# Ternary weights on two engines: GpSimd makes the first comparison, VectorE the second

## The reference

```
x = x + 0.5 * ffn0(ln(x))      # int weights: (w - 128) * scale, silu(gate) * up, down;  hidden 704
x = x + attn0(ln(x))           # 16 heads of 16, rotary, causal
x = x + 0.5 * ffn0(ln(x))
x = x + 0.5 * ffn1(ln(x))      # ternary weights: sigmoid(x1) * x2, then w3
x = x + attn1(ln(x))           # 16 query heads on 4 key heads, ALiBi, causal
x = x + 0.5 * ffn1(ln(x))
```

```
gamma = mean(abs(w));  q = clip(round(w / (gamma + 1e-8)), -1, 1)
```

## Time and profile before

| | |
|---|---|
| median of 3 runs | 553.93 us (552.02 to 555.36) |
| the profiled execution | 552.14 us, its span 550.4 us |
| TensorE clock granted | 1.000 over the span |
| TensorE busy | 530.6 us (96%), 5060 products |
| VectorE busy | 456.1 us (83%) |
| ScalarE busy | 401.3 us (73%) |
| GpSimd busy | 340.8 us (62%) |
| share of the DMA queue q1 | 16.4% of 16 engines |

### The profile page before, as it was taken

How to read it: one execution, slowest core, us unless ns; L and a number is a source line. 1 busy time by engine, 2 the same in 40 slices (tenths; PEclk the granted TensorE clock), 3 DMA queues, 4 the chain that set the end, 5 groups by cost and what they waited for, 6 DMA issues and landing times.

```text
span 550.4 us, 12977 instructions
## 1 busy us (share of the span) xinstructions
PE 530.6 (96%) x5060; PEld 302.9 (55%) x5060; DVE 456.1 (83%) x816; ACT 401.3 (73%) x603; POOL 340.8 (62%) x427
## 2 busy tenths in 40 slices
PE   8999798999999999999899999999999999999997
PEld 6676444445554654566446564465455654654664
DVE  5999999998989797699987969879997779783363
ACT  5978594878777698775886848788769676969443
POOL 2549896975987797673664364552855626545634
PEclk9999999999999999999999999999999999999999
DMA  8900110302130100410110120010211011101211
GB/s 324 355 1 2 58 58 2 116 23 62 41 103 18 43 1 2 157 42 20 63 43 2 42 83 22 22 43 6 75 36 43 1 42 64 52 2 62 80 58 38
DMA packets 22573, 31.76 MB, mean 58 GB/s; under 512 B 9408, under 2 KB 10816, under 8 KB 22360
## 3 DMA queue, kind: packets, MB, share of 16 engines
q1 hardware_dynamic: 22512, 30.94, 16.4%
HBM read 13.75 MB, written 2.36 MB: 29 GB/s over the span
## 4 chain that ended last, share of the span: by engine, by line
PE 71%; DVE 17%; ACT 4%; issue 3%; POOL 2%; SPq 1%; DMA 0%; DVEq 0%; POOLq 0%; ACTq 0%
PE PS L597 22%; PE PS L621 12%; PE PS L708 10%; PE PS L688 5%; PE PS L673 5%; DVE MX L1064 5%; PE PS L639 4%; PE PS L723 4%; PE PS L580 3%; PE PS L544 2%; PE PS L559 2%; ACT PB L850 2%; PE PS L655 2%; DVE MX L1060 1%; DVE ST L875 1%
## 5 line engine op out<-in xcount | busy, mean ns | idle before, releaser
L850 ACT ACTIVATE PB<-PS 128x1024 f32<-128x1024 f32 x160 | 158.7, 1025 | 52.9 <-PE PS L688 48.4
L1064 DVE TENSOR_REDUCE MX<-PS 128x2 f16<-128x1024 f32 (+2 forms) x192 | 158.3, 865 | 13.8 <-PE PS L544 13.1
L597 PE MATMUL PS<-XT,WGU 128*128 128x512 f16 x660 | 156.9, 380 | 4.6 <-DVE QF L1042 3.0
L1140 POOL TENSOR_TENSOR HH<-TH,HH 128x512 f16<-128x512 f32 x71 | 82.5, 1173 | 69.0 <-ACT HH L818 69.0
L1168 POOL TENSOR_SCALAR_AFFINE_SELECT PB<-PB 128x512 f32<-128x512 f32 (+1 forms) x140 | 73.8, 552 | 48.1 <-ACT PB L850 47.9
L597 PEld LDWEIGHTS PS<-XT,WGU 128*128 128x128 f16 x660 | 59.6, 98 | 75.9 <-issue 7.8
L621 PE MATMUL PS<-WD,HH 128*128 128x256 f16 x660 | 78.2, 273 | 0.4 <-POOL HH L1140 0.2
L708 PE MATMUL PS<-PB,V 128*32 128x512 f32 (+3 forms) x1024 | 75.3, 435 | 0.8 <-ACT PB L850 0.3
L621 PEld LDWEIGHTS PS<-WD,HH 128*128 128x128 f16 x660 | 62.6, 98 | 13.3 <-issue 3.3
L818 ACT ACTIVATE HH<-TH 128x512 f16<-128x512 f32 (+1 forms) x86 | 52.9, 628 | 20.2 <-PE PS L621 6.9
L673 PE MATMUL PS<-SK,SQ 63*128 63x256 f16 (+3 forms) x512 | 59.5, 299 | 5.3 <-DVE MX L1064 2.6
(11 more groups left out here) (119 smaller groups left out, 777.7 us busy)
## 6 DMA issues: line engine op xcount, KB each, us to landing
SQ<-QPB SPq DMA_DIRECT2D x24, 256.0 KB, 2.5
OC<-OT SPq DMA_DIRECT2D x16, 256.0 KB, 2.4
RB<-scratch SPq DMA_DIRECT2D x64, 64.0 KB, 2.3
SK<-QPB SPq DMA_DIRECT2D x12, 256.0 KB, 2.4
SQ<-MT SPq DMA_DIRECT2D x128, 1.0 KB
out<-X SPq DMA_DIRECT2D x8, 256.0 KB, 2.1
PB<-gu SPq DMA_DIRECT2D x2, 704.0 KB, 6.1
LATE<-gu SPq DMA_DIRECT2D x2, 704.0 KB, 14.5
```

Of the source, the lines that this page charges most:

```text
L597: m = e.matmul(o[:, :], WGU[l][:, k, col:col + P], rows_of(f)[j][:, k, :], start=j == 0 and k == 0, stop=j == 1 and k == 1)
L850: e.activation(PB[Q % 2][:, j, :, :], two_banks("s", i), ACT.Exp, scale=0.25).then_inc(a_exp, 1)
L1064: e.tensor_reduce(mx[:, :, pr, t], o[:, :, col:col + (t + 1) * P], AX.X, ALU.max, negate=True).then_inc(a_max, 1)
L1140: e.tensor_tensor(hh[1][:, s * T:(s + 1) * T], value_of(j)[0], hh[0][:, s * T:(s + 1) * T], ALU.subtract).then_inc(f_lo, 1)
```

## The change

GpSimd gets a new letter t, four times in its string. t0 and t1 do what L949 did, t2 and t3 what the two L966 did. They count on a new semaphore p_td. VectorE's w5, w6, w13 and w14 keep the second comparison with the subtraction and wait for p_td. t1 waits for w5 (both use TD), and t3 for w13 (both use TB). As six instructions leave p_dve's count, all later values fall: 14 becomes 12, 30 becomes 24, and so on. All five strings and the banks are new, with the same pieces in them but for the four t.

```diff
@@ ORDER (the first part of each string; all of it is new)
 "sp":
-        "kkrrkrkrDSrRDSRrrkDSkrRrDSRrrrkDSRkDSRrlrkkrDrSRrDSRrkklrDrSRrDSrRrkkrDrSRrDSRrDrkSkrDRSrRrrODSRDSOR"
+        "kkrrrkkrDSrRDSRrrkDrkSRrDSRrrDrkSkRDSRlrrkkrDrSrRDSRrkklrrDrSRDrSRrrkkrrDSrDSRRrrkkDSrDRSrRrrDOOSRDSR"
...
 "pe":
-        "zzzzzzzttzgGgggGGgGtzztgzGzagGgddddggGztzzgzGtGuugGaqqvgddgdvdqgGgqgtGGGguuGtqqqzmmmgmmgqmmdmmGsdsms"
+        "zzzzzzzttzgggGGgGgGGgztztzzadggdddGggGtgGGGuutgzqgqaggGddqdzdggzvgzqGGGGvuuttqqqmmgmzmmqmgdmmdsmsdms"
...
 "dve":
-        "NXgwttNhhkhhNhtwwwtwhwhwdwwdwhnhNtwhkwuuhthpqwpqwdwdpnhqpqhhkhuuhhqpttqpmmmsmhmsxmmmpmqdmpxmhqmmmsmx"
-        "mdmkmshhmnmxmmsmhmmxcmsmmmhmcmxmmmuumpqpqmxomoNdmppmqtqtcmshsxhsdhmkmmsmhmmxsmshmhmnmcdxmmuudNqpqpmm"
+        "NXwgttNhhkhhNhhwwwtwtwhdwdhnhwwhwhkuwuttpwhqpwNwhdpqwdnpkqhqhhhhuutpqtqpmmmmmsxmspmmqdmhpmqxmmhmmdmx"
+        "msmkmhsmhnmxmmshmmcmxmsmmmhmcxmmmuummpqmqxpomoNmpmpmtqxtqscdhsskhdhsmmmhmmxsmhshmmncmmxdmmuudmNpqmpq"
...
 "pool":
-        "wwwrrhrhhhhddewhwhhhshasraqdqdseasaqqhhshahhswaqqsffasfadfqdqffhfhffwehfffcfhffChcCsfsaafrfqqssaaqqd"
+        "wwwrrhhhhhtrtddhewwhhhshatrqstsdadqesaaqqhhhsahshaqsqadwfffsafqqdfffhwffehfffhhcfhffCcCsfasqffrassqa"
...
@@ vector_program, letter w
                     elif i <= 6:
...
-                        w.wait_ge(p_dve, 10 + 2 * k)
-                        e.tensor_scalar(td, src, GS[:, 5:6], None, ALU.is_lt).then_inc(p_dve, 1)
-                        w.wait_ge(p_dve, 11 + 2 * k)
+                        w.wait_ge(p_dve, 10)
+                        w.wait_ge(p_td, k + 1)
                         e.scalar_tensor_tensor(WD[1][:, c0:c1, :].rearrange("p c n -> p (c n)"), src, GS[:, 2:3],
                                                td, ALU.is_gt, ALU.subtract).then_inc(p_dve, 1)
...
                         k = i - 13
-                        w.wait_ge(p_dve, 22 + 4 * k)
+                        w.wait_ge(p_dve, 20)
                         for u in range(2):
-                            e.tensor_scalar(TB[u], rgu[k][:, u * HID:(u + 1) * HID], GS[:, 3 + u:4 + u], None,
-                                            ALU.is_lt).then_inc(p_dve, 1)
-                        for u in range(2):
-                            w.wait_ge(p_dve, 22 + 4 * k + u + 1)
+                            w.wait_ge(p_td, 2 + 2 * k + u + 1)
                             e.scalar_tensor_tensor(WGU[1][:, k, u * HID:(u + 1) * HID], rgu[k][:, u * HID:(u + 1) * HID],
                                                    GS[:, u:u + 1], TB[u], ALU.is_gt, ALU.subtract).then_inc(p_dve, 1)
@@ pool_program
+                elif c == "t":
+
+                    if i < 2:
+                        c0, c1 = ((0, 4), (4, 6))[i]
+                        w.wait_ge(l_w3, 32)
+                        w.wait_ge(p_dve, 10 + i)
+                        e.tensor_scalar(TD[:, 0:(c1 - c0) * D], rd[i].rearrange("p c n -> p (c n)"), GS[:, 5:6], None,
+                                        ALU.is_lt).then_inc(p_td, 1)
+                    else:
+                        k = i - 2
+                        w.wait_ge(l_w1, 32)
+                        w.wait_ge(p_dve, 20 + 2 * k)
+                        for u in range(2):
+                            e.tensor_scalar(TB[u], rgu[k][:, u * HID:(u + 1) * HID], GS[:, 3 + u:4 + u], None,
+                                            ALU.is_lt).then_inc(p_td, 1)
```

More of the change, by code:

```diff
@@ new lines @@
+        "GmsmdsmmsgsmmpmssgmsGsGmsspsmGmsmgmpsmsssmgmmsGmmpsmsvmssvmmsuummpqssmqoosmoossqsmdqmmdttpsgggsddssG"
+        "GgsmmpmsGmsgmmsgsGGmpmssvmsdmsdmsmvududmsqqmspoottomggosssgGGqsmggGsmmpssmGgsmtGqtpsssgddddssGggpmmm"
+        "GvgmgGmmvguGGmuoooomsqsmmqqsmdmmsddsmdsmsmssmmspmmsmttsspssgggGGgmmsgGgGGsmmpmstdtdmsmddsmgggpsmGgGu"
+        "vguGssqsmqGgsmqGmspmmddosmoddsmsososmmmpmttssmggssgGGmsspmmsgGgmsgGsmGmsmpmssdvmmsddssmdtsmspmstooom"
+        "mggoguGuGsqssmqgsmqGggmsGGmspmmsdmsdmsmddsmspsmmssmpssmttvmgggGGsmsgGgGgGmstmddmssddtmmsppmsoougugsm"
@@ new lines @@
+    "act":
+        "wXxxTwttthhtXthhtwhhxxkwttXhwhtwthtYhykyxxhtthtkQwtXtkvtQkhtYQyyQxxvhkhhtkhTQhtQweekweQewheeehQtoeee"
+        "teeeoeehthoeeeeteYhoeehveevecyyoceeeQeeeXxxQoettQQteheetehoheeteethhhcoeeveeYyeycevXoxxetQteetheheQt"
+        "theXoeehetxhhxQeoeetQeetthhovthYchvtytcyheQeQheeQeeeeeeoXexxeeoeettthhthtehtheXheoxxeetttYhoetvyhyte"
+        "eehcQQhetchQeheoeeeeXoxxeetteetheehoehttetehhehoeeXveceeexecoxeYttytyhehQeeQhetQttehhehoeeeeeoeeeXoe"
+        "xxeXtttvheehhtththhxeeecxcoeYoeyytteQeeQtQehheeeoetXohthveteeeexhhoxceceeteeetthhhXoeeteeteeeeethxxh"
+        "oocththhtcthththhXxxtththhtthhth",
@@ L141 @@
+        "frfffhfhffhhhrcCcCebffhffhhhhfffddffrrhhhhhccffCfeCffbfhfbffrhchhhCcCfffrhfffhfffchhhCchChhhhrhhhhh",
     "banks":
[L142 to L145 removed]
@@ new lines @@
+        "2563026016405240572404270125203642160721620547126351751303157015372014620474216034602475301570172351"
+        "0427240672540251252406240625251370513407345236402367420546130231656045724073025106240621523571532035"
+        "1365613062461450735107316546025260425306742604270257051352603604236514625130427401357013567415306156"
+        "3106124612640624062016305231670563107316560342604375032602405246026043673150365613502463047207054026"
+        "40265402620545027250632563105310635013762047025410636036721504710565142401240260374",
@@ L249, in macaron_kernel @@
         l_ali = [sem(f"l_ali{z}") for z in range(2)]
-        p_act, p_pool, p_dve, p_pe, p_set, p_tab, p_sc, p_gu = (sem(f"p_{n}") for n in ("act", "pool", "dve", "pe", "set", "tab", "sc", "gu"))
+        p_act, p_pool, p_dve, p_pe, p_set, p_tab, p_sc, p_gu, p_td = (sem(f"p_{n}") for n in ("act", "pool", "dve", "pe", "set", "tab", "sc", "gu", "td"))
         f_ln, f_ve, f_mean, f_rt, f_off, f_xn, f_xd = (sem(f"f_{n}") for n in ("ln", "ve", "mean", "rt", "off", "xn", "xd"))
@@ L431, in wait_read @@
             elif c == "a":
-                w.wait_ge(p_dve, (8, 20)[i])
+                w.wait_ge(p_dve, (8, 18)[i])
             elif c == "m":
@@ L589, in tensor_program @@
                     else:
-                        w.wait_ge(p_dve, 30)
+                        w.wait_ge(p_dve, 24)
                     wait_bank(w, c, i)
```

50 lines of the change are left out of this document (17 added, 33 removed).

## The result

| | before | changed |
|---|---|---|
| median, same chip | 552.97 us (4 runs) | 565.96 us (4 runs) |
| ratio, 95% interval | | 1.0224 (1.0195 to 1.0253) |
| profiled execution, its span | 552.14, 550.4 | 566.76, 565.0 |
| first row maximum starts | 78.59 | 86.57 |
| last row maximum starts | 494.90 | 507.14 |

The forecast was 551.9 us, 547.5 to 557.8. The two traces show where the 14.6 us between the spans arise: 8.0 before the first maximum, 4.2 more by the last one, 2.4 behind it.

What follows compares the result with a forecast made beforehand. VectorE's backlog, with GpSimd 0.4 us behind, was taken to bound the front, TensorE the part from 200 us. Gains of 1.4 + 0.3 + 0.3 = 2.0 us gave 550.1 profiled, 551.9 as median; range 547.5 to 557.8.

Steps and rivals of the forecast that it cites:

- (a): Front, VectorE: three |w| reductions go behind the first attention's row statistics, which come some 2.4 us earlier.
- (b): Front, GpSimd: one piece done earlier in idle time, so the first rotation starts at 45.7, not 49.14.
- (c): GpSimd from first rotation to last low part of rotated keys and queries: ends at 73.7, 1.4 us earlier.
- (d): End of the front: VectorE gives back 3 to 4 of 6.15 us as idle time; first product at 76.6.
- (e): From the first product to 107 us: VectorE's maxima are the chain, and the 1.4 us lead is carried.
- (g): Later seams (263 us, near 333, 383, 490), same work in other orders: 0.3 us gained, -3 to +3.
- Rival 2: Front, first rotation to last low part: GpSimd becomes the bound, second steps stand behind it; 557.0 us, chance 0.14.
- The prediction's first sign of it: VectorE operation on 2 elements took 0.98 us beside GpSimd work, on one element 0.15 without: the engines exclude each other.
- (f): At 122 us: a VectorE piece moves ahead, so SyncE issues a DMA sooner; 0.3 us gained (0 to 0.6).
- rival 3: Behind the front: the later orders outweigh it; 549.5 or 557 us, chance 0.22, of which 0.08 slower.
- rival 1: Front: GpSimd fits the comparisons in and the whole 6.15 us arrive; 547.8 us, chance 0.15.

Runs made afterwards that it cites:

- e3: The changed kernel with each GpSimd comparison over its first 64 columns only, the rest of the mask a constant 0; 557.01 us, ratio 1.0073.
- e6: The kernel before with GpSimd and VectorE instruction forms on 704 elements added behind all its work, alone and side by side; no kernel time given.
- e1: The kernel before with the new orders only, VectorE keeping all comparisons; 558.67 us, ratio 1.0100.
- e5: The kernel before with the new orders only from about 105 us on, VectorE keeping its comparisons; 558.02 us, ratio 1.0094.
- e2: The changed kernel with the old orders, GpSimd's four comparison letters put in; 564.12 us, ratio 1.0199.
- e9: The kernel before with VectorE's gate and up comparisons and second steps moved late, to 151 and 187 us; 556.41 us, ratio 1.0063.
- e10: As e9, but the gate and up comparisons on GpSimd at later places where it has room; 554.92 us, ratio 1.0033.
- e8: The kernel before with only the last 14 letters of SyncE's string new; 553.22 us, ratio 1.0007.

## Why the prediction was wrong, step by step

| step | forecast | changed kernel | e3 (comparisons of 0.44 us) |
|---|---|---|---|
| comparison of 704 | 0.82 (0.81 to 1.6) | 2.04 | 0.44 |
| (a) n0 starts (36.45 before) | 2.4 earlier | 37.44, 1.0 later | 34.45, 2.0 earlier |
| (b) s0 starts | 45.7 | 50.12 | 46.32 |
| (c) q3 ends | 73.7 (to 76.8) | 83.37 | 72.97 |
| (d) first m product | 76.6 | 86.08 | 75.63 |
| (e) to (g), behind it | 0.6 gained | 6.6 lost | 5.7 lost |

n0 before is this row of VectorE's timeline; the row at 38.67, with the row sums behind it, is N3:

```profile
36.45 1.40 DVE L875 BATCH_NORM_STATS2 ST<-X 128x6 f32<-128x256 f32 x4
```

The forecast span was 548.4 us and the measured one 565.0, 16.6 us more. The first product is 9.5 us later than forecast (86.08 for 76.6), and 7.2 us more are lost behind it. Two terms carry these: the price of the comparison in the front, and the later orders behind it.

**The first term that failed: the comparison's price.** "A comparison with a per-partition threshold has one input tile, so I take 0.82", from the triangular cut. On GpSimd the number of input tiles is no guide across operations: the cut takes 642 ns for 512 elements, the comparison 1570. The upper bound failed too, which is the worse fault: 1.6 was worked out from the two-input operation, on the thought that a one-input one could not cost more. It costs 2.04 to the 1.67 measured in e6. From 64, 704 and 1024 elements (0.44, 2.04, 2.85) it is 2.5 ns an element and 0.28 us fixed.

**What follows from it.** Rival 2 named this mechanism and the point from which it decides, 1.2 us; its sign was right, and its size, 557.0, hung on the same bound. The four comparisons ahead of q3 cost 4 x 1.22 = 4.9 us more than forecast, and two things were in neither sum. The first pair was to gain "next to nothing (0 to 0.6 us)", with waits of VectorE of about 0.5 us each; they are 2.53 and 1.57 us, at the head of a queue without slack, 3.1 more. And the long TensorE waits behind VectorE were not covered by warm-up products, and the clock fell to 0.50 behind them, 2.4 us by the first maximum. The three make 10.4 us, an estimate since they overlap, for the 9.7 by which q3 is late.

**Step (c), the rows beside the comparisons:** q1 takes 1.16 us in the changed kernel, 1.81 before, as the step had it. But before it stood beside VectorE's second steps (59.89 to 63.61) and not beside its comparisons, and the stretch didn't go with them: GpSimd's addition at 68.54 takes 1.91 us where others take 1.27. The second steps take 0.95, 0.95, 1.54 and 1.94 us, 1.6 more than four times 0.95 in all; rival 2's 1.4 for them was near.

**The exclusion.** The prediction's first sign of it, 0.98 us on 2 elements beside GpSimd work and 0.15 "without it", doesn't hold: GpSimd was at work at 26.21 us too, with two subtractions that end at 26.38:

```profile
24.11 2.27 POOL L1140 TENSOR_TENSOR HH<-PB,HH 128x512 f16<-128x512 f32 x2
```

The changed kernel has better rows. The second step on 512 elements takes 1.75 us (34.51) beside GpSimd's addition of 1.27 (34.44), where it takes 0.74 in e3, and ends 0.55 us behind its end, just as k12 does. The one of 1.94 (67.39) stands beside a two-tile product of 1.26 (67.32). These fit an exclusion for the whole of GpSimd's instruction. Beside GpSimd's comparisons it is otherwise: the second step at 56.80 takes 0.95 us inside the pair that starts at 54.11, and in e6 four lose 4.85 - 3.9 = 0.9 us together beside comparisons of 2.04. So whole exclusion is seen beside GpSimd's two-tile operations and not beside its tensor_scalar; why, no run here tells.

**Step (d):** the 3 to 4 us of VectorE's idle time between 50 and 66 us are there (0.48 + 3.46); those ahead of 40 us were put too low (above), and the waits for GpSimd's X come behind 66 us (1.23 us at 70.56, 1.02 at 72.94).

**The second term that failed: (e) to (g), the later orders.** Forecast 0.6 gained, (g) "with -3 to +3"; measured about 5 lost in e1 and e5, and 5.7 behind the front in e3. About 1 us arises near 110, where (e) carried the lead and (f) gained; 1 to 2 are k12 next to a GpSimd addition; 2 to 3 lie between 490 and 516 us, in part with the late landing, and are not explained. The point that "TensorE is at 98% there, so little is there to win" held for wins alone; rival 3's losing side should have had more than 0.08. At e3's price of 0.44 us the time is 557.0, just inside the forecast's range; at the forecast's own 0.82 it would be about 559, an estimate on the line from e3 to the changed kernel, outside it. So by this estimate either term alone would have missed the range; e2, with the old orders, shows it for the price.

**The rest.** The whole 6.15 us (rival 1) were never to be had: e9 takes more than that off VectorE and gains 3.3, with TensorE and GpSimd full in that stretch. Its 15% were too many.

Of the 12.4 us, 8.4 are the comparisons' duration, 2.4 to 2.9 of these by way of the clock. The other 4 are what the later orders lose (5.7 in e3's trace, k12 among it) less the 2.4 that the front would gain with cheap comparisons; the traces of single executions and the medians differ here by some tenths.

## What to carry to other kernels

Before an operation is moved to another engine, its price there has to come from the same form of instruction on that engine; where the trace has none, the bound is not the next row that looks costlier, and a probe behind the kernel's work settles it in one run. A step that is split over two engines costs the first engine a wait each time, whole where its queue is full, so it belongs where the receiving engine can be far ahead (e10), not on the chain. And new orders that come with a change are to be timed alone: here they were 5 us, and one letter beside the wrong instruction was 1 to 2 of them.

## What the runs showed that was not expected

- GpSimd's tensor_scalar takes 1.97 to 2.06 us for 128x704, for is_lt, mult and max, with a constant or a per-partition operand, to f16 or f32: more than its own two-input subtraction (1.67) and 3.5 times VectorE's 0.59.
- A 64-partition subtraction of two SBUF tiles on VectorE took 2.76 us beside a GpSimd addition of 2.36, shut out whole, and a second step 1.75 for 0.74 beside one of 1.27; four second steps beside GpSimd comparisons lost 0.9 us together.
- TensorE's granted clock was 0.50 (1.2 GHz) for 3.4 us behind idle times of 2.19 and 5.19 us; behind the same wait of 2.96 us at 68 us it was 1.00 in the trace of before and 0.51 in that of e8. Over the executions of before, one such fall goes with 1.7 us.
- The landing of the same small DMA near 505 us took 2.17 to 4.26 us in kernels whose SyncE order is the same there, and the lag grew by about 2 us more where it was long.
